# Linear attention: the key blocks turned by VectorE's 32x32 stream transpose in place of TensorE's transpose

## What is computed

```python
qkv = silu(layernorm(x) @ qkv_w.T)            # 32 heads of 64 units
q, k, v = split(qkv)
for each block of tokens:
    aw = einsum('bhid,bhjd->bhij', qi, ki) * dd        # scores times decay
    intra = einsum('bhij,bhjd->bhid', aw, vi)
    inter = einsum('bhid,bhde->bhie', qi * qd, state)
    state = state * bd + einsum('bhsd,bhse->bhde', ki * kd, vi)
x = x + sigmoid(gate) * rmsnorm(intra + inter) @ out_w.T
```

## Time and profile before

| | us |
|---|---|
| runs of the kernel | 1087.49, 1088.51, 1088.69 |
| median | 1088.51 |
| the profiled execution, its time | 1088.0 |
| its span in the trace | 1086.3 |
| TensorE busy in the span | 1043.9 (96%) |
| VectorE busy | 596.5 (55%) |
| ScalarE busy | 616.2 (57%) |
| GpSimd busy | 491.1 (45%) |

### The profile page before, as it was taken

How to read it: one execution, slowest core, us unless ns; L and a number is a source line. 1 busy time by engine, 2 the same in 40 slices (tenths; PEclk the granted TensorE clock), 3 DMA queues, 4 the chain that set the end, 5 groups by cost and what they waited for, 6 DMA issues and landing times. The chain is left out here.

```text
span 1086.3 us, 33515 instructions
## 1 busy us (share of the span) xinstructions
PE 1043.9 (96%) x14384; PEld 822.8 (76%) x14384; DVE 596.5 (55%) x1327; ACT 616.2 (57%) x1168; POOL 491.1 (45%) x527
## 2 busy tenths in 40 slices
PE   4999999999999999999999989988899999999998
PEld 3888888888888988888888878866544444455787
DVE  5243343434343353645444673598877787876433
ACT  4544444444443555555554666776577777767763
POOL 1454454455353564655554544864233333221346
PEclk9999999999999999999999999999999999999999
DMA  3100100101001011102102220058622222200001
GB/s 136 58 3 2 59 2 4 57 2 51 16 3 50 18 31 65 32 24 73 31 18 101 88 69 1 1 126 223 131 53 54 51 47 51 53 3 2 1 20 59
DMA packets 19613, 50.77 MB, mean 47 GB/s; under 512 B 2687, under 2 KB 13759, under 8 KB 16575
## 3 DMA queue, kind: packets, MB, share of 16 engines
q1 hardware_dynamic: 19470, 48.67, 16.2%
HBM read 37.71 MB, written 10.75 MB: 45 GB/s over the span
## 5 line engine op out<-in xcount | busy, mean ns | idle before, releaser
L1898 DVE TENSOR_REDUCE aa_mx<-aa_S 128x1 f32<-128x640 f32 (+1 forms) x192 | 173.4, 952 | 42.6 <-PE aa_S L1619 41.4
L518 DVE SCALAR_TENSOR_TENSOR la_y<-la_g,la_O 128x512 f32<-128x512 f32 x64 | 41.1, 684 | 234.5 <-PE la_O L704 234.5
L1807 ACT ACTIVATE aa_PT<-keep 128x512 f32<-128x512 f32 (+1 forms) x203 | 110.5, 582 | 41.3 <-PE keep L1643 39.9
L614 PE MATMUL la_R<-a_hTh,WF 128*128 128x512 f32 x384 | 128.9, 401 | 4.4 <-DVE a_hTl L160 4.4
L1542 POOL TENSOR_SCALAR_AFFINE_SELECT aa_PT<-aa_PT 128x256 f32<-128x256 f32 (+1 forms) x112 | 49.5, 442 | 177.0 <-ACT aa_PT L1807 173.8
L298 POOL TENSOR_TENSOR la_qd<-q,la_C 128x512 f32<-128x512 f32 x64 | 81.2, 1290 | 95.3 <-PE la_O L704 95.3
L311 POOL TENSOR_TENSOR la_yl<-la_y,la_yh 128x512 fp32r<-128x512 f32 x62 | 79.2, 1300 | 87.8 <-ACT la_yh L393 87.8
L361 ACT ACTIVATE q<-la_R 128x512 f32<-128x512 f32 x64 | 38.3, 599 | 116.9 <-PE la_R L614 116.9
L525 DVE TENSOR_TENSOR X<-la_R,X 128x512 f32<-128x512 f32 x64 | 44.2, 691 | 93.8 <-PE la_R L614 93.8
L1087 POOL TENSOR_TENSOR f_fl<-f_f,f_fh 128x512 fp32r<-128x512 f32 x48 | 61.8, 1298 | 62.7 <-ACT f_fh L954 62.4
L614 PEld LDWEIGHTS la_R<-a_hTh,WF 128*128 128x128 f32 x384 | 73.2, 191 | 21.4 <-DVE a_hTl L160 4.8
(11 more groups left out here) (290 smaller groups left out, 2768.7 us busy)
## 6 DMA issues: line engine op xcount, KB each, us to landing
la_Wraw<-w_quads_dram SPq DMA_DIRECT2D x7, 1280.0 KB, 5.6
aa_stacks<-k_parts SPq DMA_DIRECT2D x16, 256.0 KB, 6.6
q_parts<-aa_QP SPq DMA_DIRECT2D x8, 384.0 KB, 4.8
aa_stacks<-q_parts SPq DMA_DIRECT2D x8, 384.0 KB, 4.7
k_parts<-aa_KP SPq DMA_DIRECT2D x8, 384.0 KB, 4.8
qw_w<-w_ffn_dram SPq DMA_DIRECT2D x12, 192.0 KB, 2.4
q_ffn<-qw_w SPq DMA_DIRECT2D x12, 192.0 KB, 1.9
X<-hidden_dram SPq DMA_DIRECT2D x4, 512.0 KB, 7.2
```

The source lines that it names most:

```text
L614: m = pe.matmul(out, a, b, start=n == 0, stop=n == len(pairs) - 1)
L1807: act.activation(PT[:, (NM2 * g + b) % NPT, h:h + nh, 0:w], ST[at % NB][:, 0:nh * w].rearrange("p (h q) -> p h q", h=nh), ACT.Exp, scale=S ...
L1898: dve.reduce_max(out, src, AXX).then_inc(s1_free, 1)
```

## The change

VectorE turns the keys of unit j+2 within unit j, with its stream transpose, which transposes blocks of 32x32. One instruction takes 32 partitions (a quarter of the 128, `QUAD`) and 8 blocks of 32 columns, and writes them to 32 partitions of `kd`; 16 such instructions (`NTURN`) turn a unit. The 16 run through the four output quarters for each of the four input quarters. They read `k` in SBUF and write `kd` in SBUF. ScalarE's `keys` then scales `kd` in place. Eight of the 16 stand ahead of `sums(j, 0)`, two between the two sums, six behind `sums(j, 1)` and ahead of `rounded` and `split`. TensorE keeps its transposes for unit 0 and for unit 31 (the last), so 30 of 32 sets leave it.

```diff
+QUAD, NTURN = 32, 16
...
-            def keys(i, j, pr):
+            def keys(i, j, pr, banks=None):
...
-                    kbv = Y[h][:, pr * GC * LD:(pr + 1) * GC * LD].rearrange("p (c n) -> p c n", c=GC)
+                    kbv = kdv[:, :, h * LD:(h + 1) * LD]
+                    if banks is not None:
+                        kbv = banks[h][:, pr * GC * LD:(pr + 1) * GC * LD].rearrange("p (c n) -> p c n", c=GC)
...
+            def turned_keys(i, j, a, b):
+                n, m = step(i, j)
+                if a == 0:
+                    dve.wait_ge(silu_ok, 64 * i + 8 * j)
+                for at in range(a, b):
+                    f, t = slice(at // 4 * QUAD, (at // 4 + 1) * QUAD), slice(at % 4 * QUAD, (at % 4 + 1) * QUAD)
+                    ins = dve.transpose(kd[t].rearrange("p r (c n) -> p r c n", c=GC)[:, :, :, f],
+                                        k[f, m % 2].rearrange("p r (c n) -> p r c n", c=GC)[:, :, :, t])
+                if b == NTURN:
+                    ins.then_inc(kb_ok, 1)
...
+                ahead = has(last, j, 2) and not (last and j == 5)
+                if ahead:
+                    turned_keys(i, j + 2, 0, 8)
                 if not (last and j == 6):
                     for n in range(2):
                         sums(i, j, n)
+                        if ahead:
+                            turned_keys(i, j + 2, (8, 10)[n], (10, NTURN)[n])
...
             masks(0, 1)
+            turned_keys(0, 1, 0, NTURN)
...
-                if has(last, j, 1):
-                    turned_keys((j + 1) % 8)
+                if last and j == 6:
+                    turned_keys(7)
                 carried(j)
```

More of the change, by code:

```diff
@@ L383, in unit @@
                     for pr in range(2):
-                        keys(*step(i, j + 1), pr)
+                        keys(*step(i, j + 1), pr, Y if last and j == 6 else None)
                 if last and j == 6:
@@ L457, in _ @@
             for pr in range(2):
-                keys(0, 0, pr)
+                keys(0, 0, pr, Y)
                 evict(0, 1, "k", pr, 6 + pr)
```

## The result

The changed kernel takes 1111.7 us (median of 4 runs, 1110.72 to 1113.31), the kernel before 1088.6 in the same session (4 runs, 1087.49 to 1089.64): a ratio of 1.0214, 95% interval 1.0196 to 1.0232. It is slower by 23.1 us, where 13.5 had been forecast. The profiled execution took 1113.31 us with a span of 1111.4, 25.1 us more than the span before.

A forecast was written before the change was run, and what follows sets the result against it. TensorE, never waiting in the linear attention, was taken as the bound. Gain -19.2, late sums +24.0 and late v weights +9.0 gave +13.8 us on the profiled 1088.0, so 1101.8, or 1102 us against the median; range 1083 to 1117 us.

The forecast's parts named there:

- The gain: TensorE's stream in the linear attention: 30 of 32 transpose sets leave, 0.64 us each, 19.2 us gained if nothing waits.
- T: Time of one VectorE stream transpose of 256 f32 columns on 32 partitions: 0.44 us, taken without overlap.
- The rival with 0.33: VectorE's transposes overlap, 0.33 to 0.37 us each; at 0.33 net -7.7, 1081 us, faster; chance 0.20.
- Term A: TensorE's "q" projection waits for VectorE's late second sum, about 2 us in units with a chunk: 24.0 us in all.
- the average of 0.15 over the plain units: Mean wait of "q" for the sums, taken between 0.26 (unit 13) and 0.02 (unit 0): 2.4 us over 16 units.
- Term B: TensorE's "v" waits for weight pieces late behind the 16 transposes, 1.1 or 1.5 us in seven units: 9.0 us.
- What cost nothing: Turned keys ready ahead of state_sums, GpSimd's decayed moved by up to 2.5 us, gated still in time: nothing charged.
- rival 5: TensorE's clock falls in the new waits; held within the range's upper end, no chance of its own given.
- Rival 2: VectorE's transpose takes 0.37 to 0.39 us, waits and gain cancel within 2 us: 1087 to 1091 us; chance 0.09.
- rival 3: VectorE's transpose takes two passes or a slow f32 path, 0.69 us: net +96, 1185 us; chance 0.04.
- rival 4: VectorE's added transposes delay nothing, full gain, 1069 us; needs a transpose below 0.24 us; chance 0.03.
- has room wherever it counts: Wording of rival 4 about VectorE: the full gain, 1069 us; chance 0.03.

The follow-up runs named there:

- the probe: Kernel before plus 18 added stream transposes of 32 x 256, within and across quarters; starts 0.33 to 0.34 us apart within a quarter, 0.45 across; no kernel time given.
- one transpose: Changed kernel with one of a unit's 16 stream transposes left, its result not the reference's; 1074.68 us, ratio 0.9866 to the kernel before.
- plain units only: Changed kernel, but VectorE turns keys in the 16 plain units alone, TensorE from unit 18's keys on; 1087.43 us, ratio 0.9977 to the kernel before.
- the best version: Changed kernel with all 16 transposes behind the weight pieces, three units ahead, second kd slot, next stage's loads held back; 1070.42 us, ratio 0.9828 to before.

## Why the prediction was right in kind and short in size

**The gain.** 0.64 us a set holds: -0.64 in nearly every unit of the versions that make nothing late. For the changed kernel the ledger takes 18.9 us, 29 such units and the 0.37 by which unit 0 starts earlier, against 19.2. The 0.37 are not evidence for the thirtieth set: the probe kernel, which takes nothing off TensorE's stream, starts unit 0 0.65 us earlier than before.

**T.** 0.446 us measured, 0.44 forecast, from no overlap. The rival with 0.33, which would have made the kernel faster, falls by the quarters alone: 0.33 is what a transpose takes when nothing changes its quarter. That the working hit 0.44 so closely is in part luck. It took 0.41 for an instruction of 256 columns and added 0.03 for the first block; in the probe a transpose within its quarter lasts 0.39 us alone (0.72 - 0.33), and 0.43 to 0.44 only where it changes the quarter.

**Term A** was put at 24.0 us and measured 27.4. With a chunk, odd units lose 1.50 + 0.64 = 2.14 (forecast 2.00) and even ones 1.28 + 0.64 = 1.92 (1.79), 22.4 us in eleven. The plain units lose 4.2 in sixteen, where 2.4 stood, and units 16 and 28 0.8 together (0.6). The waits themselves were forecast to 0.03 us: the second half of "q" starts 2.02 us later in its unit than before in unit 17 and 1.81 in unit 20 (forecast 2.00 and 1.79), 0.29 in unit 13 (0.26) and 0.03 in unit 8 (0.02). The term that was left out is the restart: the matmul behind the stop holds the next back by 0.34 us and not 0.23, 0.11 us in each such unit. In unit 13 the second sum ends at 311.49 + 0.69 = 312.18, about 0.23 us after TensorE wants it; with the hand-over and the restart that is the 0.41 that odd plain units lose. The other step that was short is the average of 0.15 over the plain units, drawn between 0.26 and 0.02: it kept the even units' 0.1 about right and put the odd ones at a third of their 0.41, and units 1 and 9, where VectorE's masks end 0.2 us later than in units 5 and 13, at a quarter of their 0.60 to 0.63.

**Term B** was put at 9.0 us and measured 10.2: 1.04 to 1.33 in four plain units (forecast 1.1), 4.9 together, and 3.05 - 1.28 = 1.77 in three chunk units (1.5). The trace of unit 18 shows 1.65 of wait and the restart's 0.11.

**What was left out.** TensorE's stops in units 29 and 30, 1.6 us, of a kind for which no row of before was read. And 4.8 us behind the linear attention in the profiled execution. The 32 us from the start of the softmax attention's scores, in the kernel before:

```profile
745.00:777.00 32.00, 25.60 (x187) 17.49 (x187) 26.65 (x31) 14.61 (x28) 9.34 (x20) 0.95 0.60 150
```

The same in the changed kernel:

```profile
766.00:798.00 32.00, 27.74 (x164) 19.36 (x165) 24.95 (x28) 13.15 (x25) 8.94 (x19) 0.73 0.58 148
```

TensorE is busy longer with fewer matmuls, at a granted clock of 0.73 instead of 0.95; this part, up to the first of the products with the values (`aa_SO<-aa_PT,aa_V`), takes 34.4 us and not 32.3. Over the ten profiled executions it takes 30.8 to 31.2 us at a clock of 1.00 (the probe, one transpose, plain units only, the best version), 32.3 to 32.6 at 0.89 to 0.95 (before among them) and 34.4 only here. The probe, with the whole stream, has 1.00 and before 0.95, so this follows the execution and not the length of the stream; the profiled execution is also the slowest of the changed kernel's four. A second place is the entry of the last feed-forward network, in the kernel before:

```profile
1008.00:1013.00 5.00, 4.29 (x23) 3.73 (x24) 2.15 (x6) 3.48 (x5) 0.00 (x0) 1.00 0.00 0
```

And in the changed kernel:

```profile
1033.00:1038.00 5.00, 5.00 (x19) 4.07 (x17) 2.10 (x3) 3.33 (x5) 0.00 (x0) 0.66 0.00 0
```

The work ahead of it is the same in both, with the clock at 1.00 in the ten microseconds before; here it is 0.66 instead of 1.00, and 1.4 us are lost. From the first `f_T` matmul (1008.71 before, 1032.38 now) to the first of `keep<-e_hTh` it took 17.6 to 17.8 us in the profiled executions of all eight kernels with a shorter TensorE stream, and 16.2 in before and in the probe. Why the clock falls at this place was not settled. The remaining 1.2 us of the 4.8 lie ahead of the scores.

The ledger reads -18.9 + 27.4 + 10.2 + 1.6 = +20.3 us to unit 31 (it must close, since the terms are the lengths of the units, split by kind; what tests it are the waits in the trace and the runs without them), where -19.2 + 24.0 + 9.0 = +13.8 was forecast, and 4.8 behind it make the 25.1 of the span. Of the 9.6 us by which the difference of the medians lies above the forecast, some 6.5 are in the linear attention and 1.4 at the second place. The rest is about 1.7 us, and the changed kernel's own runs lie 2.6 apart.

**What cost nothing** did: no wait at `state_sums`, and ScalarE's `keys` waited 0.4 us at the most. GpSimd's products were on time, and the clock held 1.00 through the waits, so rival 5 fell within the attention. Rival 2, rival 3 and rival 4 fell with T. That VectorE "has room wherever it counts" came true in another order of the same instructions.

## What to carry to other kernels

When work moves from a full engine to one with much idle time, ask first what stands behind it in that engine's queue and what the full engine needs from there: here the same 480 instructions cost 23 us ahead of two sums, and behind them they gave 14, or 19 with one load held back. A second slot for the result, so that the work can be done a unit earlier and last in the queue, is the first thing to look for. Price each wait of a saturated TensorE with its restart, here 0.11 us, and read the windows of more than one unit of each kind before averaging.

## What the runs showed of the hardware that was not expected

- The quarter decides the pitch of VectorE's transposes of 32 x 256: 0.33 us within a quarter, 0.45 when input or output moves to another. The price of the hold, 0.12 us, is a third of the 0.33.
- TensorE stopped in the middle of a group of like matmuls, for 2.60 us, with the DMA engines 0.55 to 0.65 busy just ahead, and did not once those loads were held back, nor with the same loads in the kernel before; the changed kernel, with the loads and a shorter stream, has 0.65 us at this place. The page lists a DMA kind "instruction" (`q8 instruction: 110, 1.80, 0.7%` in the changed kernel), and 34 of 38 such stops end 1.2 to 1.6 us after one of its packets. That TensorE waits for late instructions fits all of this and is not shown by a run of its own.
- Behind that stop of 2.60 us the granted clock was 0.93 and then 0.73 in the stretches of 5 us, while with waits of 1.65 us in unit after unit it stayed at 1.00.
